# One routing batch for each of eight groups, earlier sends, and two slot tables in place of three in a two-layer mixer and expert kernel

## The reference

```python
def block(x, l):
    x = x + mixer[l](layernorm(x))           # l = 0: attention, l = 1: mix
    return x + experts(layernorm(x))

# attention: q, k = elu(x W) + 1; v = x W_v; running sums over time
S = S + k_t v_t^T;  z = z + k_t
o_t = (S q_t) / max(z . q_t, 1e-6);  out = o W_o

# mix: prev_t = x_(t-1) + d * prev_(t-1), d = exp(-exp(time_decay))
r = sigmoid(r_in Wr^T);  out = (r * (v_in Wv^T)) Wo^T

# experts: 8 of them, one for each token
gate, e = max and argmax of softmax(x router_W + router_b)
out = gate * (relu(x W1[e] + b1[e]) W2[e] + b2[e])     # 128 -> 512 -> 128
```

## Time and profile before

| | |
|---|---|
| three runs | 371.5, 380.53, 377.52 us (median 377.52) |
| the profiled execution | 372.29 us, of which the span of the trace is 370.5 |
| busy in the span | PE 298.7 us (81%), DVE 248.7 (67%), POOL 204.2 (55%), ACT 135.7 (37%) |
| mean granted TensorE clock | 0.926 of full speed |

### The profile page before, as it was taken

How to read it: one execution, slowest core, us unless ns; L and a number is a source line. 1 busy time by engine, 2 the same in 40 slices (tenths; PEclk the granted TensorE clock), 3 DMA queues, 4 the chain that set the end, 5 groups by cost and what they waited for, 6 DMA issues and landing times.

```text
span 370.5 us, 8996 instructions
## 1 busy us (share of the span) xinstructions
PE 298.7 (81%) x2133; PEld 254.2 (69%) x2133; DVE 248.7 (67%) x1005; ACT 135.7 (37%) x431; POOL 204.2 (55%) x248
## 2 busy tenths in 40 slices
PE   2789999879864799999997799985575398999970
PEld 1357666556753699999944688864465388999970
DVE  4677889886772367777617999980486066777750
ACT  3654664321422244443403555320232143444420
POOL 4854478776537445545525557887155634554450
PEclk9999999986998599999999999997599779999996
DMA  7992000005664478776325000115366357777600
GB/s 201 240 191 25 0 32 31 29 31 139 172 158 130 116 187 228 201 223 170 97 71 159 0 3 29 37 52 147 89 162 171 95 130 217 194 215 192 180 32 0
DMA packets 42610, 44.22 MB, mean 119 GB/s; under 512 B 7120, under 2 KB 29905, under 8 KB 42560
## 3 DMA queue, kind: packets, MB, share of 16 engines
q10 hardware_dynamic: 11808, 20.71, 21.0%
q1 hardware_dynamic: 26176, 14.39, 17.7%
q0 software_dynamic: 4576, 8.54, 6.5%
HBM read 33.06 MB, written 11.53 MB: 120 GB/s over the span
## 4 chain that ended last, share of the span: by engine, by line
PE 57%; DVE 9%; another core or an unknown queue 9%; issue 7%; ACT 6%; POOL 3%; DMA 2%; DVEq 2%; ACTq 2%; POOLq 0%; SPq 0%
PE pair L1389 15%; PE pair L1378 11%; PE bank L1378 5%; PE pair L1315 3%; PE pair L1319 3%; PE pair L1206 2%; PE bank L1368 2%; PE pair L1267 2%; PE pair L1336 2%; PE pair L1252 2%; PE pair L1188 2%; PE pair L1196 2%; PE pair L1230 2%; POOL rstd L426 2%
## 5 line engine op out<-in xcount | busy, mean ns | idle before, releaser
L1389 PE MATMUL pair<-w2s,hT 128*128 x624 | 87.6, 285 | 4.7 <-issue 3.1
L1389 PEld LDWEIGHTS pair<-w2s,hT 128*128 128x128 f32 x624 | 79.5, 200 | 7.3 <-issue 7.1
L467 POOL DMA_INDIRECT sorted<-rows,place x64 | 65.7, 1027 | 23.2 <-issue 15.8
L1378 PE MATMUL pair<-xsT,w1s 128*128 128x128 f32 x448 | 67.8, 290 | 10.1 <-ACT xsT L670 6.3
L1378 PEld LDWEIGHTS pair<-xsT,w1s 128*128 128x128 f32 x448 | 60.7, 205 | 11.0 <-ACT xsT L670 6.9
L670 ACT COPY xsT<-bank 128x128 f32<-128x128 f32 x78 | 20.7, 265 | 119.7 <-PE bank L1368 78.4
L480 POOL DMA_INDIRECT out<-ys,xs x39 | 38.1, 977 | 41.4 <-issue 22.7
L480 POOL DMA_INDIRECT x_mid<-ys,xs x39 | 38.0, 974 | 40.6 <-issue 22.4
L1072 DVE SCALAR_TENSOR_TENSOR ys<-pair,xs 128x128 f32<-128x128 f32 x78 | 27.3, 350 | 34.0 <-remote 15.9
L1061 DVE TENSOR_SCALAR hT<-pair,w1s 128x128 f32<-128x128 f32 x130 | 40.4, 344 | 8.3 <-remote 7.8
L1053 DVE SCALAR_TENSOR_TENSOR xs<-b2b,xs 128x128 f32<-128x128 f32 x78 | 27.4, 352 | 22.0 <-DVE xsn L1045 17.3
(11 more groups left out here) (158 smaller groups left out, 486.4 us busy)
## 6 DMA issues: line engine op xcount, KB each, us to landing
w1s<-in_L_ffn_W_b ACTq DMA_DIRECT2D x78, 258.0 KB
xs<-sorted SPq DMA_DIRECT2D x78, 66.0 KB
rows<-in_L_attn_a_x SPq DMA_DIRECT2D x8, 256.0 KB, 4.1
w2s<-in_L_ffn_W SPq DMA_DIRECT2D x8, 256.0 KB
rows<-x_mid SPq DMA_DIRECT2D x8, 256.0 KB, 5.3
sorted<-pad SPq DMA_DIRECT2D x30, 66.0 KB, 3.5
sorted<-rows,place POOLq DMA_INDIRECT x64
x_mid<-ys,xs POOLq DMA_INDIRECT x39
```

Of the source, the lines that this page charges most:

```text
L467: pool.indirect_dma_start(sorted_rows[l], bass.IndirectOffsetOnAxis(ap=place[:, t:t + 1], axis=0), rows[:, t, :], None).then_inc(s_sent[l] ...
L1378: mm = nc.tensor.matmul(bank[2 + 2 * half + i % 2][:, c * P:(c + 1) * P], w1s[i % NW][:, f:f + P], xsT[i % NB][:], start=True, stop=True)
L1389: mm = nc.tensor.matmul(bank[6 + i % 2][:, 0:P], hT[i % NB][:, c], w2s[:, bass.ds(e, 1), c, :].rearrange("p o d -> p (o d)"), start=(c == ...
```

## The change

1. ROUTE_BATCHES: every group is a batch, so groups 6 and 7 are routed and sent apart. The last batch has four sends in place of eight.
2. STAGES: the first table comes after batch 4 and makes 13 slots known, the last after batch 7 makes 26 known. The middle table and its part 3 (with `taken`) are gone.
3. CHOOSE_AT, COUNT_AT, PLACE_AT, TABLE_AT go from 2, 4, 4, 5 to 3, 5, 5, 7.
4. Adding epsilon to the variance moves from POOL to ACT (row_veps).
5. In slots 0 and 1 of an expert layer ACT takes all four chunks of the hidden layer (ALL = 2), in place of three.
6. In attention each engine's slot has a new order; choose is done for group k - 2 (before k - 3), placed and count for k - 3 (before k - 4), and sends start up to a slot earlier. In mix, placed and the sends are done for k - 2 (before k - 3). In mix PE's matmuls of a slot are cut into rows, first half and second half of the scan, with count and the transposes between.
7. The keep_clock(2) behind attention and the one before experts(1) are gone; those between the layers stay. project_out of the last group and count of the last batch but one move behind turn(0) and first(0) of the experts; the last group's mix, logits and positions move into the start of experts(1).

```diff
-ROUTE_BATCHES = [[0], [1], [2], [3], [4], [5], [6, 7]]
+ROUTE_BATCHES = [[g] for g in range(8)]
-STAGES = [(3, 9), (5, 8), (6, 22)]
+STAGES = [(4, 13), (7, 26)]
-CHOOSE_AT, COUNT_AT, PLACE_AT, TABLE_AT = 2, 4, 4, 5
+CHOOSE_AT, COUNT_AT, PLACE_AT, TABLE_AT = 3, 5, 5, 7
+ALL, WIDE = 2, 13
...
@@ POOL, row_scales
-                nc.gpsimd.tensor_scalar(veps2[:, t], column(GATE, t), EPS, None, ALU.add).then_inc(S["rs2"], 1)
+                pool.wait_ge(S["ve2"], b + 1)
...
@@ POOL, experts
                     scatter(l, i)
+                    if i == 1:
+                        row_scales((AS, BS)[l], LASTB)
                     if i == PLACE_AT:
@@ POOL, attention
-                if k - 4 >= 0:
-                    send(0, AS, k - 4, 0)
-                if 0 <= k - 1 < NG:
-                    old_logits(k - 1)
                 if k - 4 >= 0:
                     send(0, AS, k - 4, 1)
-            send(0, AS, 5)
-            row_scales(AS, LASTB)
+                if k - 2 >= 0:
+                    old_logits(k - 2)
+                    row_scales(AS, k - 2)
+                if k - 3 >= 0:
+                    send(0, AS, k - 3, 0)
+            send(0, AS, LASTG - 2, 1)
+            old_logits(LASTG)
+            send(0, AS, LASTG - 1)
@@ POOL, mix
-                if (b := batch_ending(ROUTE_BATCHES, k - 1)) is not None and b < LASTB:
-                    row_scales(BS, b)
-                if k - 3 >= 0:
-                    send(1, BS, k - 3)
-            row_scales(BS, LASTB)
+                if 0 <= k - 1 < LASTB:
+                    row_scales(BS, k - 1)
+                if k - 2 >= 0:
+                    send(1, BS, k - 2)
@@ DVE, attention
-                if 0 <= k - 2 < NG:
+
+                if 0 <= k - 2:
                     denominators(k - 2)
-                if k < NG:
-                    phi(k)
+                    add_attention(k - 2)
                 if 0 <= k - 1 < NG:
                     mask_scores(k - 1)
...
@@ DVE, experts
                     if i == 0:
+                        if l == 1:
+                            keep_logits()
+                            placed(1, BS, LASTB - 1)
+                        dve.wait_ge(S["xnew"], NG)
                         moments(S, 2, LASTG)
+                    if i == 1:
                         slot_table(l, 0, (3,))
-                    if i == 1:
-                        slot_table(l, 1, (0, 1, 2))
-                    if i == TABLE_AT - 2:
-                        slot_table(l, 1, (3,))
@@ PE, attention and between mix and experts
-                if k == NG:
-
-                    pe.wait_ge(s_w2, 16 * (1 + E))
-                    keep_clock(2)
-                    count(AS, LASTB - 1, bank[2])
-                    project_out(LASTG)
...
-            keep_clock(2)
             experts(1)
```

288 lines of the change are left out of this document (166 added, 122 removed).

## The result

| | before | the changed kernel |
|---|---|---|
| runs | 371.5, 380.53, 377.52, 376.03 us | 389.3, 384.35, 387.62, 384.05 us |
| median | 376.77 us | 385.99 us |
| profiled execution, its span | 372.29, 370.5 us | 389.3, 387.6 us |

What follows compares the result with a forecast made beforehand. It took VectorE's pace in the first expert slots and stalls beside POOL's last-batch sends as the bound. First layer -4.6 and mix with second layer +0.9 gave -3.7 us: 368.6 by profile, 371 by median; range 359 to 381.

Steps and rivals of the forecast that it cites:

- Attention: Attention slots: 8.6 to 8.7 us each, +0.3 over six slots, so 1.2 to 2 us longer, of which 1.2 was taken.
- The way into the experts: From attention to the first expert slot: second(0) at 94.2 in place of 95.74, -1.5 us with attention's loss in it.
- The first slots: First expert slots, at VectorE's pace: 1.9 us less VectorE work, last batch's positions at about 109.1 in place of 111.24, -2.1.
- The last batch: Last batch of an expert layer: four sends for eight, 5.0 us less burst; late matmuls through at 118.7, before 125.8.
- rival C: The stalls aren't the sends': no 5.0 us in either layer, new waits come; 375 by profile, 377.5 by median; chance 0.20.
- A: Last batch: four sends leave no stall, the eight pads take 9 us; 358.6 by profile, 361 by median; chance 0.21.
- B: Pads with landing take the full 20.1 us, everything stands 4.6 us per layer; 380.6 by profile, 383 by median; chance 0.17.
- The new waits: Before slot 13: ScalarE waits 2.75 us per layer for its weights; pads take 12 us, its rows come at 128.5.
- Mix and second layer: Mix slots gain nothing, the second layer's first load comes 1.2 us later, and +0.9 us was taken in all.
- The scale: Whole kernel: 371 is 374.9, the middle of four runs, less 3.7; the 2% mark was 370 on the median's scale.

Runs made afterwards that it cites:

- a1: The changed kernel with TensorE's count(k-3) moved behind transpose_x(k+1) in the attention slot: 377.94 us, 1.007 of before.
- a2: The changed kernel with POOL's z_dot_q(k-1) moved behind the second half of send(k-4) in attention: 379.84 us, 1.011 of before.
- a3: The changed kernel with both attention edits, count behind transpose_x and z_dot_q behind the sends: 370.65 us, 0.985 of before.
- d1: The kernel of a3 with the slots in three stages, (3, 9), (5, 8), (7, 22), and the middle table back: 344.19 us, 1.003 of before.
- e2: The kernel of a3 unaltered, run again at the level without late results: 356.93 us beside 343.06, 1.034 of before.

## Why the prediction was wrong, step by step

- **Attention** failed, and it decides the result: "+0.3 over six slots, 1.2 to 2 us" measured +15.0. I counted VectorE's work from the denominators to read_inter and took for granted that they begin 3.1 us into the slot. I never asked when count's one-hot is there. In both kernels the choice of a group comes in one slot and its count in the next. But before, the moments and scan_z stood behind the one-hot in VectorE's slot, and it was ready 0.8 us ahead of count. Now it is the last thing in VectorE's slot, behind moments, state, placed, phi and the scan, while count is still at the start of TensorE's next slot, ahead of score. That loop and z_dot_q beside the one-hot share the loss: one edit alone brings attention back by 4.4 us (a1) or 5.6 (a2), both by 14.3 (a3). z_dot_q I had not looked for; of POOL in attention I had said only that it is busy two thirds of the time.
- **The way into the experts**: from read_inter's end to second(0) 9.4 us (100.16 to 109.57), before 10.6. -1.2, where I had -2.7. A late result of 2.87 us lies in it.
- **The first slots**: slots 0 to 4 take 2.7 us each (109.57 to 120.44) in place of 3.3, with the late result of 3.80 us inside, so VectorE's pace was not the whole of it. Whether the missing table or ScalarE's fourth chunk, which I took at nothing, gave the gain isn't tested. But the positions come one slot later (PLACE_AT is 5): `ends` begins 16.6 us behind second(0), before 15.4. My 109.1 also doesn't come out of its own terms, since 111.24 - 1.5 - 1.9 is 107.8.
- **The last batch**: two pieces of the chain, 2.67 and 4.35 us, in place of 6.73 and 5.12, so -4.8; I had -5.0. That speaks against rival C for the chip of that result: four sends fewer, 4.8 us less. But in the first layer as a whole the late results did not shrink, by the new ones in the first slots, which are no term of my sum. And with a batch for each group, positions and STAGES all changed at once, no run shows that the number of sends does it. The Trainium skill's page that C leant on, "SBUF — State Buffer", section "Who interferes with whom", has PE and ACT wait on no one. Late results of 3.48 us twice on ScalarE, beside sends, are not what I read from it; what holds them up no row names. At the other level there is no stall, so it isn't tested there.
- **Rivals A and B**: four sends did leave a stall and the pads took 12.61 us, not A's 9. B's sign, the first load over 18 us behind the positions, did not come: it was 15.9 (126.33 to 142.20).
- **The new waits**: I had 2.75 us for the weights, rows at 19.4 us behind the positions and 12 for the pads. Measured: ScalarE's wait is 5.87 us, the rows come 18.3 us behind (126.33 to 144.59). VectorE still waits 3.55 us for them, B's mechanism with less than B's delay. From the positions to second(11) it is 21.7 us (126.33 to 148.0), and I had 21.8. So the first layer's miss, second(11) 47.9 us behind read_inter and not 44.6 (before 50.4), lies in the entry and the first slots. What the waits cost with no stall to hide them I had no price for; d1 against e2 gives about 5 us a layer at slots 9 to 12.
- **Mix and second layer**: the first send comes 18.0 us into the mix, 4.6 earlier, and groups are 6.9 us apart, as I had it; the first load is +2.8 where I had +1.2. Behind it I had no loss; the slots to the last add_y take 1.8 us more, so the layer is +4.6 from the mix's start where I had +0.9, with 5.90 us of ScalarE for weights and 3.97 of VectorE for rows once more. The first send and SP's load (the fifth group's first send starts at 259.85):

```profile
232.18 1.45 POOL L493 DMA_INDIRECT sorted<-rows,place  x1 [0.72 <-POOL rows L467]
...
268.01 13.91 SPq L360 DMA_DIRECT2D xs<-sorted  x13
```

- **The scale**: in the chances I set my 371, on the middle of 374.9, against a 2% mark of 370 that belongs to the median 377.52; on 374.9 the mark is 367.4.

With attention mended (a3) the kernel is at 370.65 us, and I had 371. That is not the forecast come true, since a3 isn't this change, and the agreement is in part luck. In its trace attention is +0.7 and the first layer -2.0 where I had +1.2 and -5.8; the way to the second layer's first load is +2.8, and the slots behind it -3.9.

## What to carry to other kernels

When a change moves a step one slot forward on one engine, take each engine's order and look for loops: what stands ahead of the waited-for step, and what stands behind the waiting one. A result that moves to the end of one engine's slot, while its reader stays at the start of the other's next one, can put both engines' work into one chain that is paid in every slot. Beside an instruction with two SBUF operands on VectorE look at what POOL does at that moment. And a margin (slots between a table and its first use) has to be measured against the time from the last count to the rows' landing, in a state without the stall that hides it.

## What the runs showed of the hardware

- The same program took 370 to 384 us in some groups of runs and 341 to 346 us in others. Most of the difference is results of matmuls that reach VectorE and ScalarE late, in pieces of up to 7.5 us, in stretches where POOL issues indirect DMAs: 9% of the chain or none. Chip number 1 stands at both levels, so if the number means one chip it is a state of it; the runs don't tell what brings it about, nor what in the sends does it.
- With late results SP's issue of eight pads beside the sends took 12.3 to 13.6 us beside four sends and 15.5 to 17 beside eight; without them 8.2 to 9.1, beside four or eight.
- A VectorE operation of 0.19 us took 1.83 to 1.96 us beside a POOL operation of 1.27 us, which itself was not longer; beside a send of POOL's it took 0.19.
